# A DLRM tower on one core: gathers that wait for set points of TensorE's program

## The reference, cut to what matters

```python
e = jnp.stack([tbl_0[ids[:, 0]], tbl_1[ids[:, 1]], ..., tbl_26[ids[:, 26]]], axis=1)
dot = jnp.einsum('bnd,bmd->bnm', e, e)
idx = [i * 27 + j for j in range(1, 27) for i in range(j)]
z = dot.reshape(2048, 27 * 27)[:, idx]
h = jnp.concatenate([z, dense_ctx], axis=1)
h = jnp.maximum(h @ W_top1 + b_top1, 0.0)      # 367 x 512
h = jnp.maximum(h @ W_top2 + b_top2, 0.0)      # 512 x 256
y = h @ W_top3                                 # 256 x 1
```

## Time and profile before

| what | us |
|---|---|
| median of three runs | 709.78 (707.19 to 711.47) |
| the profiled execution, its own time | 705.33 |
| its span, first to last instruction | 703.5 |
| PE busy | 407.6 (58%) |
| POOL busy (gathers) | 246.3 (35%) |
| mean granted TensorE clock | 0.765 of full |

### The profile page before, as it was taken

The page is one execution under the profiler, slowest core; times in us unless marked ns, Lnnn a source line. Parts: engine busy times, 40 slices in busy tenths (PEclk is TensorE's granted clock), DMA queues, the critical chain, the costliest instruction groups (busy, mean ns, idle before and its releaser), DMA issues.

```text
span 703.5 us, 15274 instructions
## 1 busy us (share of the span) xinstructions
PE 407.6 (58%) x6218; PEld 360.3 (51%) x6218; DVE 272.8 (39%) x804; ACT 142.0 (20%) x189; POOL 246.3 (35%) x264
## 2 busy tenths in 40 slices
PE   3327501892529724497245945179552892639875
PEld 3316401891429723396235935069441791529854
DVE  6506222781308603185032833028421581308211
ACT  3307210140103301023011321002210240103421
POOL 6750457007440347103561064600546007440000
PEclk9759755796759957599576976659766896759997
DMA  7921512011111211102111111110211111110000
GB/s 211 263 61 39 153 42 69 19 56 54 33 35 32 75 37 45 48 4 73 42 46 46 44 52 30 48 34 18 76 31 49 36 53 54 30 36 2 2 2 1
DMA packets 22295, 36.58 MB, mean 52 GB/s; under 512 B 12662, under 2 KB 13310, under 8 KB 22252
## 3 DMA queue, kind: packets, MB, share of 16 engines
q1 hardware_dynamic: 13996, 19.01, 9.3%
q0 software_dynamic: 8256, 16.92, 8.5%
HBM read 35.90 MB, written 0.01 MB: 51 GB/s over the span
## 4 chain that ended last, share of the span: by engine, by line
PE 52%; issue 32%; another core or an unknown queue 7%; DVE 3%; DMA 2%; ACT 2%; SPq 1%; DVEq 0%; ACTq 0%
PE emb_ps L670 20%; PE gram_ps L714 13%; PE mlp_ps L733 5%; PE emb_ps L706 4%; PE mlp_ps L747 3%; DMA embT<-in_tbl 2%; PE emb_ps L686 2%; DVE onehot L564 1%; PE mlp_ps L776 1%; PE mlp_ps L755 1%; PE mlp_ps L724 1%; SPq L271 1%; PE mlp_ps L781 1%; ACT onehot L425 0%
## 5 line engine op out<-in xcount | busy, mean ns | idle before, releaser
L391 POOL DMA_INDIRECT rows<-in_tbl,idx x256 | 244.0, 953 | 378.4 <-PE emb_ps L706 256.7
L714 PE MATMUL gram_ps<-embT 128*32 128x26 f32 x4096 | 97.0, 220 | 235.1 <-issue 214.6
L564 DVE TENSOR_SCALAR onehot<-ids_b,row_of 128x256 fp32r<-128x256 int32 x694 | 193.5, 356 | 44.9 <-PE emb_ps L670 37.5
L714 PEld LDWEIGHTS gram_ps<-embT 128*32 128x32 f32 x4096 | 74.1, 140 | 261.3 <-issue 240.0
L670 PE MATMUL emb_ps<-onehot,parts 125*128 125x256 f32 x1280 | 176.1, 298 | 48.0 <-issue 31.5
L670 PEld LDWEIGHTS emb_ps<-onehot,parts 125*128 125x128 f32 x1280 | 168.4, 203 | 52.3 <-issue 48.4
L576 DVE STREAM_TRANSPOSE turned<-gram_ps 128x832 f32<-128x832 f32 x16 | 16.8, 1050 | 309.4 <-PE gram_ps L714 284.8
L436 ACT ACTIVATE embT<-emb_ps 128x512 f32<-128x512 f32 x40 | 48.9, 1232 | 118.9 <-PE emb_ps L670 118.9
L444 ACT ACTIVATE embT<-emb_ps 128x512 f32<-128x512 f32 x32 | 36.4, 1237 | 167.4 <-PE emb_ps L706 141.3
L570 DVE COPY embT<-emb_ps 128x512 f32<-128x512 f32 x32 | 35.4, 1185 | 28.4 <-PE emb_ps L706 28.4
L733 PE MATMUL mlp_ps<-zT,w_sb 128*128 128x256 f32 (+1 forms) x168 | 38.7, 378 | 0.0
(11 more groups left out here) (43 smaller groups left out, 115.5 us busy)
## 6 DMA issues: line engine op xcount, KB each, us to landing
ids_b<-in_ids_mm SPq DMA_DIRECT2D x8, 896.0 KB
ids_b<-in_ids_mm SPq DMA_DIRECT2D x16, 256.0 KB
rows<-in_tbl,idx POOLq DMA_INDIRECT x256
embT<-in_tbl SPq DMA_DIRECT2D x6, 448.0 KB
w_sb<-in_tbl SPq DMA_DIRECT2D x2, 448.0 KB
turned<-in_tbl SPq DMA_DIRECT2D x1, 560.0 KB
w_sb<-in_W_top SPq DMA_DIRECT2D x1, 512.0 KB, 4.1
turned<-in_tbl SPq DMA_DIRECT2D x1, 448.0 KB
```

Source lines behind the costliest of these rows:

```text
L391: pool.indirect_dma_start(rows[:, t, n, :], None, tables[f], bass.IndirectOffsetOnAxis(idx[:, t, f:f + 1], 0), engine_sem=gathers_written) ...
L564: last = nc.vector.tensor_scalar(onehot[:, k % OH, c, :], ids_b[:, of, :], row_of[:, first + c:first + c + 1], None, ALU.is_equal)
L714: last = nc.tensor.matmul(gram_ps[q * COLS:(q + 1) * COLS, g * COLS:g * COLS + NJ], embT[:, t, at:at + COLS], embT[:, t, at:at + NJ], star ...
```

## The change

POOL's program gets a second wait ahead of each group of four gathers, `keep_step`. No other engine's program is touched, and no instruction is taken away. With p the pass whose rows are gathered, the points are, for tile 0: group 0 none beyond what was there; group 1 the end of tile 0's last transposes in pass p - 1; group 2 the end of the Gram of tile 0 in p - 1; group 3 the end of tile 1's last transposes in p - 1. For tile 1: group 0 the end of the Gram of tile 1 in p - 1; groups 1, 2 and 3 the ends of lookup jobs 0, 1 and 2 of pass p itself. In pass 0, where no pass lies before, tile 0's group 3 waits for the first table's lookup and tile 1's groups for job 0, the first table of job 1, job 1 and job 2.

```diff
@@ -377,6 +377,32 @@
                 past(pool, gathers_written, n - 1)
                 pool.sem_inc(pool_waited, 1)
 
+            def keep_step(p, t, k):
+
+
+                if isinstance(p, int) and p == 0:
+                    if t == 0 and k == 3:
+                        pool.wait_ge(s_looked, 1)
+                    elif t and k == 0:
+                        pool.wait_ge(emb_filled, 1)
+                    elif t and k == 1:
+                        pool.wait_ge(s_looked, 2)
+                    elif t:
+                        pool.wait_ge(emb_filled, k)
+                elif t == 0:
+                    if k == 1:
+                        pool.wait_ge(emb_filled, (p - 1) * JOBS + row_job(0, NT - 1) + 1)
+                    elif k == 2:
+                        pool.wait_ge(gram_filled, (p - 1) * TILES + 1)
+                    elif k == 3:
+                        pool.wait_ge(emb_filled, (p - 1) * JOBS + row_job(1, NT - 1) + 1)
+                elif k == 0:
+                    pool.wait_ge(gram_filled, p * TILES)
+                else:
+
+                    pool.wait_ge(emb_filled, p * JOBS + k)
+                pool.sem_inc(pool_waited, 1)
+
             def body(p, first, last):
                 extra = 0 if first else TILES
                 for t in range(TILES):
@@ -385,6 +411,7 @@
 
                         past(pool, emb_filled, (p - 1) * JOBS + row_job(t, k) + 1)
                         pool.sem_inc(pool_waited, 1)
+                        keep_step(p, t, k)
                         for n in TR[k]:
                             f = GATHERED[n]
                             one_queued((p * TILES + t) * NG + n + (TILES if first and t else extra))
```

## The result

The changed kernel takes 575.82 us, the median of four runs (573.92 to 578.39), against 710.62 for the kernel before in four runs beside it (707.19 to 712.66). The ratio is 0.811, with an interval of 0.806 to 0.816. The forecast was 625 with a range of 590 to 685: the direction was right, and the time lies 14 us under the range. The profiled execution took 578.39 us (span 576.6) against the 705.33 (703.5) on which the sum was made, so 127 us went, where 85 were expected.

A forecast was written before the change was run, and what follows sets the result against it. Runs of gathers lying on the Grams were taken to bound the kernel. 120 + 20 + 8 - 63 = 85 us off 705.3 gave 620 for the profiled execution, 625 as median, range 590 to 685.

The forecast's parts named there:

- What bounds the kernel: Runs of gathers that lie on the Grams stall PE 18 to 19 us per Gram, beside 3 to 4 of work.
- Rival D: Gathers don't cause the stall, so the time stays at 706 to 712 us; chance 0.05.
- the law: A run of n gathers frees PE 1.25 (n - 1) + 4.0 us after starting: 12.75 us for 8.
- Grams: Both tiles' Grams in passes 1 to 6: runs of 8 instead of 16 save 10.0 us each, 120 us.
- Lookups: Lookups of passes 1 to 7: tile 1's groups beside them lose 9 us a pass, 63 us (0 to 175).
- the bound of 175: Upper end of the loss in the lookups of passes 1 to 7, where 63 us were expected.
- Pass 0: Saves 20 us from the first run behind the lookups to Gram 1's end, and 8 in the first lookups.
- rival C: Short runs are free in lookups, at 2 or 3 us a pass: about 580 us; chance 0.14 (under 600).
- A: Every run stops lookups 3.4 us in, about 15 us lost a pass: about 675 us; chance 0.22.
- B: A kernel slower than before, from 20 us lost a pass; chance 0.09.

The follow-up runs named there:

- the strict wait: The kernel before, but each gather waits until its forerunner's descriptors are written, not those of the one before that: 528.11 us against 709.58.
- the kernel with the breaks: The changed kernel, with VectorE waiting for its own last one-hot after each table from pass 1 on: 563.66 us, ratio 0.794 to the kernel before.

## Why the prediction was too high, step by step

**What bounds the kernel** was right. Runs of gathers starve PE; without gathers a Gram of passes 2 to 6 has no gap. Rival D (706 to 712 us), by which gathers don't cause the stall, is out: the stalls follow the gathers' spacing, 214.6 us in all at 1.25, 58.3 at 1.75 and 28.5 at 2.30. They don't follow the instruction packets that the profile counts: 36 before and after the change (18 without gathers) and 63 with the strict wait.

**The step that failed** is the law under all terms: "By the rows above, a run of n gathers frees PE 1.25 (n - 1) + 4.0 us after its start". The 4.0 us had been read twice, both times from 16 gathers, and carried to 8 and 4 as a constant. It is a debt that grows with each gather: 1.94, 2.66, 3.99 us for 4, 8 and 16. The one row of another length, 5.2 us after 34, pointed that way, and I passed over it. The sum then erred to the same side in each term:

*Grams, 120 forecast, 135.6 measured.* Eight gathers release PE 1.34 us sooner than counted; for twelve Grams that is 16 us, as much as the difference. A Gram takes 10 to 12.8 us in most passes; 13 were given. The merging into runs of 8 was as described. Two differ, and both follow a blocked gather: Gram 0 of pass 2 takes 7.9 us (tile 0's first group had gone in the run of 15, and a run of 4 was left), that of pass 6 19.5 (beside the run of 14). Together they cost 4 us; with intact gathers the twelve Grams saved 139 us.

*Lookups, 63 lost forecast, 48.3 measured.* This is two errors against each other. With intact gathers (the kernel with the breaks) the lookups cost 213.8 - 181.2 = 32.6 us, 4.7 a pass instead of 9: the gaps of a run of 8 are 2.5 us and not 5, and clock and held-back signals 2 and not 4. No run shows the 2 us for the clock by itself. What the runs show is that PE's busy time in the lookups of passes 1 to 7 was 190.6 us with the breaks and 179.1 before, 1.6 more a pass, at a granted clock of 0.90 to 0.94 in each (before 0.84 to 1.00); in the stretch of the earlier trace rows it was 0.50 (296 to 300), and 1.00 from 303 to 312. Nor does any run show the 25 us a pass behind the bound of 175. The blocked gathers take 9 us of that away again (204.8, not 213.8), and cost 24.7 us between the lookups and Gram 0. The rows of before hardly warned of them: in its loop one-hots and gathers met only for some 2.5 us at a time (8 one-hots at 239.42 and at 268.20 in pass 2), and the longest gather of the whole trace took 1.91 us. That PE's flow lasts 8 us beside lookups and 3 to 6 beside a Gram held, but this was luck in part: the pass 0 row on which the lookups' part rested stops for ScalarE, as the kernel without gathers shows, and it has a gap of 0.87 us at 12.06, 8.6 us into the run, that the prediction left out.

*Pass 0, 28 forecast, 39.5 measured.* From the first run behind the lookups to the end of Gram 1 it is 27.5 us, where 29 were worked out. The lookups gave 17.7 us (the run starts at 61.05 and not at 78.71); I had bounded them at 16 and taken half, for no row's sake. Here the halving cost nearly 10 us.

15.6 + 14.7 + 11.5 = 42 us make up the way from 620 to the 578.4 of the profiled execution. The first, about 3 of the last and some 9 of the middle one hang on the law; with the law alone put right the forecast would have been near 597, and still 21 us above the measured time.

**The rivals.** The time is that of rival C, which had said that short runs are free beside lookups, at 2 or 3 us a pass. That its 580 lies so near is luck, since its price is off: the true price was 4.7 and, with the blocked gathers, 6.9 a pass, and the missing gain was in the Grams and in pass 0. A, and B (a kernel slower than before, from 20 us lost a pass), would have needed lookups that stop 3.4 us into a run; they stop after 8.

## What to carry to other kernels

When a stall is read from runs of one length, its constant part may be a debt that builds up: look for a row of another length before you scale it. If an engine starves beside back-to-back gathers of another, try their spacing before their placing; here one count in a wait gave 181 us and the points 135. But a spacing of 2.30 us made POOL the bound and gave only 53. After such a change compare the longest durations of each instruction with its median, and count them: four of 10 to 13.67 us against 0.95 name a new collision at once.

## What the runs showed of the hardware

Once PE's first 40 or so Gram records are gone, each indirect gather that POOL issues holds PE up for about 1.4 us, by my reading in two pieces of 0.70, whatever its bytes and rows (with half of the one 708.19 us, with half of the other 706.69, ratios 1.004 and 1.003); the sum made with 1.41 us gives the release after runs of 4 to 34 to within 0.4 us. 256 gathers, and two for the eleventh table, cost 315 us of 710, with starts 1.25 us apart. What links the two is not settled by these runs. That it is not the bytes that arrive is shown by the kernels without gathers and with half the bytes.

A gather can be held while VectorE runs one-hots without a break, 13.67 us at most here. These one-hots are comparisons with a scalar from int32 to a 4-byte float, and the gather stays held from one instruction to the next: 52 of them, 0.26 us apart, gave the 13.67 us gather no opening; a wait of VectorE for its own result after each table did, with 1.30 us for the longest gather. What the two contend for, no run here shows.

The three kernels with the strict wait and 1.75 us spread by 3.6 to 5.6% (501 to 529 us in six runs of the last, where the kernel before spread by 1.2% in 17 runs beside it), so differences under 3% between them are not told here.
